# Conditioned two-layer attention: ten second-layer groups send their output by transfers, and GpSimd inverts and divides for them

## The reference

```python
def layer0(x, cond):                      # [4, 512, 256]
    xm = rms(x) * (1 + scale(cond)) + shift(cond)
    q, k, v = split(xm @ w_qkv)           # rope on q and k
    o = softmax(q @ k.T / 4) @ v          # per head
    return o @ w_out + x

def layer1(x, emb, mask):
    xn = layer_norm(x)
    q, k, v = xn @ q_w + q_b, xn @ k_w + k_b, (xn @ v_w + v_b) * mask
    y = softmax(q @ k.T - 1e6 * (1 - mask)) @ v
    h = layer_norm(y) * (1 + scale(emb)) + shift(emb)
    return x + silu(h) @ out_w + out_b
```

## Time and profile before

| | us |
|---|---|
| median of 3 runs (490.25 to 492.41) | 490.78 |
| the profiled execution | 490.88 |
| its span, first to last instruction | 488.7 |
| PE busy | 477.4 |
| DVE busy | 385.4 |
| ACT busy | 342.1 |
| POOL busy | 313.7 |

### The profile page before, as it was taken

The page is one execution under the profiler, slowest core; times in us unless marked ns, Lnnn a source line. Parts: engine busy times, 40 slices in busy tenths (PEclk is TensorE's granted clock), DMA queues, the critical chain, the costliest instruction groups (busy, mean ns, idle before and its releaser), DMA issues.

```text
span 488.7 us, 9702 instructions
## 1 busy us (share of the span) xinstructions
PE 477.4 (98%) x3197; PEld 179.5 (37%) x3197; DVE 385.4 (79%) x989; ACT 342.1 (70%) x677; POOL 313.7 (64%) x445
## 2 busy tenths in 40 slices
PE   7999899999999999999999999999999999999996
PEld 3553322322443325332443335334333323333234
DVE  3767896999886796958886698866899999999124
ACT  2662467898667785968667785876787788777853
POOL 5569976899885996789755791859990055005501
PEclk9999999999999999999999999999999999999999
DMA  7775157454522465216502361113311121111011
GB/s 251 201 202 192 45 152 250 112 150 128 150 61 65 129 178 151 62 33 181 154 19 69 113 179 45 46 45 113 106 46 44 45 89 45 44 46 45 1 44 44
DMA packets 41577, 49.79 MB, mean 102 GB/s; under 512 B 12388, under 2 KB 34036, under 8 KB 41272
## 3 DMA queue, kind: packets, MB, share of 16 engines
q1 hardware_dynamic: 33336, 31.84, 21.8%
q0 software_dynamic: 7904, 16.03, 11.3%
q10 hardware_dynamic: 288, 1.31, 0.8%
HBM read 27.62 MB, written 19.01 MB: 95 GB/s over the span
## 4 chain that ended last, share of the span: by engine, by line
PE 79%; DVE 12%; POOL 3%; issue 2%; ACT 1%; DVEq 0%; POOLq 0%; ACTq 0%
PE bank L596 20%; PE bank L642 12%; PE bank L570 12%; PE bank L579 11%; PE bank L558 9%; DVE masked L955 7%; PE bank L653 6%; PE bank L670 5%; DVE row_max L958 2%; PE bank L627 2%; POOL XN L930 1%; PE bank L611 1%; PE bank L604 1%; ACT probs L780 1%; PE bank L727 1%
## 5 line engine op out<-in xcount | busy, mean ns | idle before, releaser
L780 ACT ACTIVATE probs<-bank 128x512 f32<-128x512 f32 x512 | 269.2, 601 | 71.1 <-PE bank L570 70.3
L958 DVE TENSOR_REDUCE row_max<-bank 128x1 f32<-128x512 f32 x256 | 159.4, 681 | 34.0 <-PE bank L579 33.7
L579 PE MATMUL bank<-k_s,q_s 64*128 64x512 f16 x512 | 178.3, 382 | 2.0 <-DVE row_max L958 1.2
L955 DVE CUSTOM_DVE_ANT_0 masked<-bank,mask_bias 128x512 bf16<-128x512 f32 x256 | 161.8, 687 | 19.3 <-PE bank L579 18.7
L558 PE MATMUL bank<-q_s,k_s 64*128 64x512 f16 x512 | 151.5, 380 | 0.3
L570 PE MATMUL bank<-shift,kx 64*128 64x512 f16 x512 | 148.8, 376 | 0.0
L596 PE MATMUL bank<-probs,v_aug 128*17 128x512 f32 x1024 | 135.4, 598 | 0.7 <-ACT probs L780 0.7
L579 PEld LDWEIGHTS bank<-k_s,q_s 64*128 64x128 f16 x512 | 46.2, 93 | 156.1 <-DVE row_max L958 70.2
L642 PE MATMUL bank<-xT,wqkv 128*128 128x512 f32 x128 | 59.6, 605 | 1.1 <-DVE xT L1096 0.6
L1236 POOL TENSOR_SCALAR scaled<-row_max 128x16 f32<-128x16 f32 x30 | 7.7, 256 | 81.4 <-DVE row_max L955 45.1
L570 PEld LDWEIGHTS bank<-shift,kx 64*128 64x128 f16 x512 | 46.8, 95 | 33.6 <-DMA shift<-shift_rows 0.4
(11 more groups left out here) (123 smaller groups left out, 478.7 us busy)
## 6 DMA issues: line engine op xcount, KB each, us to landing
q_s<-q_parts SPq DMA_DIRECT2D x32, 256.0 KB, 3.0
k_s<-k_parts SPq DMA_DIRECT2D x32, 256.0 KB, 3.7
k_parts<-parts POOLq DMA_DIRECT2D x62, 128.0 KB, 3.0
q_parts<-parts POOLq DMA_DIRECT2D x60, 128.0 KB, 3.1
X<-in_x SPq DMA_DIRECT2D x4, 512.0 KB, 7.2
O<-oT SPq DMA_DIRECT2D x64, 32.0 KB, 2.2
roped<-inverses SPq DMA_DIRECT2D x16, 128.0 KB
y<-X SPq DMA_DIRECT2D x7, 256.0 KB, 2.2
```

Source lines behind the costliest of these rows:

```text
L579: nc.tensor.matmul(bank, m.q_s[slot][rows, i, queries], m.k_s[slot][rows, i, :], start=True, stop=True).then_inc(q.d_made, 1)
L780: act.activation(m.probs[k][:, h, :], bank, ACT.Exp, scale=1.0 if s >= B * NG else float(DH) ** -0.5)\
L955: dve.tensor_tensor_reduce(m.masked[D["max", n, k, h] % ND][:, :], bank, m.mask_bias[:, b, :], 1.0, LOWEST, ALU.add, ALU.max, to)\
L958: dve.tensor_reduce(to, bank, AX.X, ALU.max).then_inc(q.d_done, 1)
```

## The change

The last six groups (26 to 31) stay as they are. Groups 16 to 25 (up to the new `SENT` = 26) go the way of layer 0: sums, raw output and inverses by SP's transfers.

- **Pool** inverts, with a power of -1 over 128x16 (`invert`), in place of DVE's reciprocal, and divides each chunk of two groups in place in `raw`. Its list from shift 19 on is written out anew: ten inverts and five divisions among the shifts, splits, bias additions and normalisations; silu and the bias additions are cut into halves in some places.
- **PE** turns a divided chunk back with four transposes (`turn_back`, pieces `back`, in ring A), so five times four in place of ten times four. **ACT** copies the result to `tokens`, which lies in the memory of the conditioning weights. **DVE** no longer inverts and multiplies for these groups; its statistics wait for the copy of the last turn back.
- **SP** issues per group seven transfers more (one of sums, four of raw output, one each of inverses out and in), and waits in `inverses_out` for Pool's invert, and in `inverses_in` for the write to have landed.
- **Pieces** move: back turns stand at steps 20 (tile 1), 21 (tile 3, ahead of the value products of the last sequence, which were in step 20), 23 (tile 3), 25 (tile 2) and 28 (tile 2). The two w_out halves of sequences 0 and 1 are paired, in step 25 and 28, tile 3; the turns of normalised tokens are a step later (23 and 27), as are two of the statistics (21 and 25). QKV chunks 2 and 3 of the last sequence in layer 0 are paired in step 1, tile 2.

```diff
+SENT = LAYER + NG * (B - 2) + NG // 2
...
-    1: (qk(0, 3, 2), (), qk(0, 3, 3), ()),
+    1: ((), (), qk(0, 3, 2, 3), ()),
...
-PIECES[20] = ((), qk(1, LAST, 2, 3), (), v(1, LAST))
-PIECES[22] = (*one(turn("f1", 0)), (), ())
-PIECES[23] = ((), (), y(1, 0)[:1], ())
-PIECES[24] = ((), (), (), y(1, 0)[1:])
-PIECES[26] = (*one(turn("f1", 1)), (), ())
-PIECES[27] = ((), (), y(1, 1)[:1], ())
-PIECES[28] = ((), (), (), y(1, 1)[1:])
...
+PIECES[20] = ((), qk(1, LAST, 2, 3) + (("back", 0, 0),), (), ())
+PIECES[21] = ((), (), (), (("back", 0, 1),) + v(1, LAST))
+PIECES[23] = (*one(turn("f1", 0)), (), (("back", 1, 0),))
+PIECES[25] = ((), (), (("back", 1, 1),), y(1, 0))
+PIECES[27] = (*one(turn("f1", 1)), (), ())
+PIECES[28] = ((), (), (("back", 2, 0),), y(1, 1))
...
-for _b in range(B - 1):
-    STATISTICS[20 + NG * _b, 3] = ("f1", _b)
+for _b, _s in enumerate((21, 25, 28)):
+    STATISTICS[_s, 3] = ("f1", _b)
...
-OUT_AT = {25: 0, 29: 1, 32: 2}
+OUT_AT = {26: 0, 29: 1, 32: 2}
...
-        if op == "output" and k == 2 and s > LAYER:
+        if op == "output" and k == 2 and s > SENT:
...
-        if op == "output" and k == 3 and 0 < s <= LAYER:
+        if op == "output" and k == 3 and 0 < s <= SENT:
...
+        m.tokens = [m.wc[:, 2 * i:2 * i + 2, :].rearrange("p k n -> p (k n)").rearrange("p (t c) -> p t c", c=C)
+                    for i in range(2)]
...
+    def turn_back(piece):
+        _, b, c = piece
+        bank = a_free(A[piece])
+        pe.wait_ge(q.divided, normalised(B + b, c))
+        for t in range(TPB):
+            last = nc.tensor.transpose(bank[:, t * P:(t + 1) * P], m.raw[b % 2][:, c, t * P:(t + 1) * P], m.ident[:, :])
+        last.then_inc(q.a_made, 1)
...
+    def back(piece):
+        _, b, c = piece
+        bank = made(A[piece])
+        if b >= 2:
+            act.wait_ge(q.xn_made, TPB * NORMAL.index(("f1", b - 2)))
+        act.activation(m.tokens[b % 2][:, :, c * P:(c + 1) * P], bank.rearrange("p (t n) -> p t n", n=P), ACT.Copy)\
+            .then_inc(q.a_done, 1)
...
-        if s == LAYER:
-            dve.wait_ge(q.inv_out, 16 * LAYER)
-        if g == 0 and pu < B + 2:
-            dve.wait_ge(q.divided, normalised(pu - 2, CT - 1))
-        if g == 0 and pu >= B + 2:
+        if s == SENT:
+            dve.wait_ge(q.inv_out, 16 * SENT)
+        if s == SENT or g == 0:
...
-        if s > LAYER:
+        if s > SENT:
...
-        dve.tensor_tensor(m.O[pu % 2][:, :, g * G * DH:(g + 1) * G * DH].rearrange("p t (h d) -> p t h d", d=DH),
+        dve.tensor_tensor(m.tokens[pu % 2][:, :, g * G * DH:(g + 1) * G * DH].rearrange("p t (h d) -> p t h d", d=DH),
...
-            dve.wait_ge(q.d_done, D["output", NG * (B + b) + NG - 1] + 1)
-            statistics(kind, b, lambda t: m.O[b % 2][:, t, :])
+            dve.wait_ge(q.a_done, max(A[piece] for piece in A if piece[:2] == ("back", b)) + 1)
+            if NG * (B + b) + NG > SENT:
+                dve.wait_ge(q.d_done, D["output", NG * (B + b) + NG - 1] + 1)
+            statistics(kind, b, lambda t: m.tokens[b % 2][:, t, :])
...
-    def add_bias(b, j):
+    def add_bias(b, j, tiles=range(2)):
...
-        for t in (2 * j, 2 * j + 1):
+        for i in tiles:
+            t = 2 * j + i
...
-    def divide(b, c):
...
-        use = USES.index(("f0", b))
-        pool.wait_ge(q.output_out, group_out(NG * b + 2 * c + 1))
-        pool.wait_ge(q.inv_in[c], 32 * (b + 1))
-        await_read(pool, q, use - 2)
-        pool.tensor_tensor(m.xT[use % 2][:, c, :], m.raw[b % 2][:, c, :], m.inverse[c][:, :], ALU.mult)\
-            .then_inc(q.divided, 1)
+    def divide(pu, c):
...
+        layer, b = divmod(pu, B)
+        pool.wait_ge(q.output_out, group_out(NG * pu + 2 * c + 1))
+        pool.wait_ge(q.inv_in[c], 32 * (pu + 1))
+        to = raw = m.raw[b % 2][:, c, :]
+        if layer == 0:
+            use = USES.index(("f0", b))
+            await_read(pool, q, use - 2)
+            to = m.xT[use % 2][:, c, :]
+        pool.tensor_tensor(to, raw, m.inverse[c][:, :], ALU.mult).then_inc(q.divided, 1)
...
+    def invert(s):
...
+        pool.wait_ge(q.sums_in, 16 * (s + 1))
+        pool.wait_ge(q.inv_out, 16 * s)
+        pool.tensor_tensor(m.inv_sum[:, :, :, :].rearrange("p t h w -> p (t h w)"), m.sums[s % 2][:, :], m.minus_one[:, :],
+                           ALU.pow).then_inc(q.inv_made, 1)
...
-    normalise(LAST)
-    add_output_bias(LAST)
-    add_bias(LAST - 1, 0)
-    add_bias(LAST - 1, 1)
-    negate(NG * LAST + 9)
-    for i in range(4):
-        split(B + LAST, i)
...
-    for b in range(LAST):
-        negate(NG * (B + b) + 6)
-        rstd("f1", b)
-        normal("f1", b)
-        if b == 0:
-            add_bias(LAST, 0)
-        negate(NG * (B + b) + 7)
-        if b == 0:
-            add_bias(LAST, 1)
-        for h in range(CT):
+    def silu(b, halves=range(CT)):
+        for h in halves:
...
-        for n in (NG * (B + b) + 8, NG * (B + b) + 9):
-            if n in POOL_SHIFTS:
-                negate(n)
...
+    pool.wait_ge(q.one_made, 1)
+    invert(16)
+    invert(17)
+    normalise(LAST)
+    divide(B, 0)
+    add_output_bias(LAST)
+    add_bias(LAST - 1, 0)
+    invert(18)
+    add_bias(LAST - 1, 1)
+    negate(21)
+    split(B + LAST, 0)
+    invert(19)
+    split(B + LAST, 1)
+    negate(22)
+    divide(B, 1)
+    invert(20)
+    split(B + LAST, 2)
+    split(B + LAST, 3)
+    negate(23)
+    rstd("f1", 0)
+    normal("f1", 0)
+    invert(21)
+    negate(24)
+    invert(22)
+    divide(B + 1, 0)
+    silu(0, (0,))
+    negate(25)
+    silu(0, (1,))
+    invert(23)
+    add_bias(LAST, 0, (0,))
+    negate(26)
+    divide(B + 1, 1)
+    add_bias(LAST, 0, (1,))
+    invert(24)
+    add_bias(LAST, 1)
+    negate(27)
+    rstd("f1", 1)
+    normal("f1", 1)
+    invert(25)
+    negate(28)
+    divide(B + 2, 0)
+    silu(1)
+    negate(29)
+    negate(GROUPS - 2)
+    rstd("f1", 2)
+    normal("f1", 2)
+    negate(GROUPS - 1)
+    silu(2)
...
-        if b >= 2:
+        if b >= B + 2:
+            sp.wait_ge(q.a_made, A["back", b - 2 - B, g // 2] + 1)
+        elif b >= 2:
...
-        if 0 < s <= LAYER:
+        if 0 < s <= SENT:
...
-        if 0 < s <= LAYER:
+        if 0 < s <= SENT:
...
-        if 0 < s <= LAYER:
+        if 0 < s <= SENT:
...
+        if LAYER < s <= SENT:
+            inverses_in(s - 1)
```

More of the change, by code:

```diff
@@ L278, in chunk_rows, with normalised @@
     return slice(G * DH * (g % 2), G * DH * (g % 2 + 1))
-def normalised(b, c):
-    return CT * b + c + 1
+def normalised(pu, c):
+    return CT * pu + c + 1
 def await_shift(engine, q, n):
@@ L384, in build @@
         m.minus_half = sb("minus_half", [P, NT])
+        m.minus_one = sb("minus_one", [P, KT * G])
         m.stats = sb("stats", [P, NT, 6])
@@ L408, in build @@
         m.k_dram = nc.dram_tensor("k_parts", [LAYERS * B, H, 2, 2, DH, S], F16, kind="Internal").ap()
-        m.inv_dram = nc.dram_tensor("inverses", [B * NG, G, S], F32, kind="Internal").ap()
+        m.inv_dram = nc.dram_tensor("inverses", [SENT, G, S], F32, kind="Internal").ap()
         def sem(name):
@@ L430, in build @@
         q.inv_made = sem("inv_made")
+        q.one_made = sem("one_made")
         q.xn_made = sem("xn_made")
@@ L752, in tensor @@
                 turn_tokens(piece)
+            if piece[0] == "back":
+                turn_back(piece)
             if piece[0] == "qk":
@@ L909, in scalar @@
                 tokens(piece)
+            if piece[0] == "back":
+                back(piece)
             if piece[0] == "qk":
@@ L1113, in last_batch @@
     def last_batch():
-        O = m.O[LAST % 2]
+        O = m.tokens[LAST % 2]
         steps = [TPB]
@@ L1173, in vector @@
                 negate(n)
-        if op == "sums":
+        if op == "sums" and at[0] < LAYER:
             invert(*at)
@@ L1180, in vector @@
                 for t in range(TPB):
-                    dve.bn_stats(m.last_stats[:, t, 0, :], m.O[LAST % 2][:, t, 0:EARLY]).then_inc(q.last_step, 1)
+                    dve.bn_stats(m.last_stats[:, t, 0, :], m.tokens[LAST % 2][:, t, 0:EARLY]).then_inc(q.last_step, 1)
         if op == "statistics":
@@ L1211, in normal @@
             await_turned(pool, q, NORMAL[n - 2])
-        src = m.O[b % 2] if kind == "f1" else m.X[:, TPB * b:TPB * b + TPB, :]
+        src = m.tokens[b % 2] if kind == "f1" else m.X[:, TPB * b:TPB * b + TPB, :]
         for t in range(TPB):
@@ L1327, in gpsimd @@
     pool.memset(m.minus_half[:, :], -0.5).then_inc(q.ident_made, 1)
+    pool.memset(m.minus_one[:, :], -1.0).then_inc(q.one_made, 1)
     pool.memset(m.ident[:, :], 0.0).then_inc(q.ident_made, 1)
```

## The result

The changed kernel takes 497.64 us (median of six runs, 496.11 to 499.34), the kernel before 490.83 beside it: a ratio of 1.013, 95% interval 1.0097 to 1.0163. It is 6.8 us slower where 2.8 us of gain were forecast, and it lies outside the range. The profiled execution took 496.11 with a span of 494.3, so it is 5.2 us above the profiled execution of before.

The account below looks back on a forecast made before the run. The prediction took PE's summed work to set each step, with DVE close behind. From 490.88 us it took 4.4 for the sum without waits and added 1.6 for new waits: 488.0 us, range 485.8 to 490.8.

Parts of the forecast that it names:

- The sum without waits: Whole kernel: transposes out -6.3, turns back +3.15, pairs -0.63, DVE -0.64, together -4.4 us.
- The pairs and DVE's 0.32: Two pieces paired save 0.21, three times; DVE's 0.32 excess is given back in two steps with statistics and a residual.
- The prediction's bound of 0.6: ACT's copies of turned-back chunks cost 0, unless one delays a score bank: then at most 0.6 us each.
- The power: Pool's power over 128x16 takes 3.0 us, extrapolated from 0.71 for two columns and 1.04 for four.
- land about 1.9 after issue: SP's transfers of sums, which Pool's powers wait for, land about 1.9 us after issue.
- PE turns it 1.36 after the mark: PE turns every shift 1.36 us after ACT's step-end mark, so shifts must start by 0.5 after it.
- just in time: Pool's splits end 14.1 us after mark 20 and step 21 takes 14.2, so shift 23 meets its slot.
- power 22 covers it: The read back of inverses lands later than other transfers, but Pool's power 22 runs meanwhile, hiding that.
- The wait for chunk (1, 0): Step 23, tile 3: PE wants the chunk at t + 16.9, Pool divides it by t + 18.4; wait some 1.5 us.
- Slower: Rival, chance 0.07: powers of 4.2 us make shifts and chunks late, 7.5 us in waits, 494 us; decides from about 3.9.
- A longer wait: Rival, chance 0.18: each 0.3 us more in a power or landing costs about 0.9; 489.7 to 490.7 us.
- No wait: Rival, chance 0.25: powers of 2.5 us or less, so PE finds chunk (1, 0) divided; 486.4 us.

Follow-up runs that it names:

- e1: The changed kernel with the ten inverts given back from Pool to DVE as reciprocals: 487.4 us, ratio 0.9931 to the kernel before.
- e8: e1's kernel, line for line, measured once more for a narrower interval: 487.74 us, ratio 0.995 to the kernel before.
- e2: The changed kernel with Pool's power of 128x16 replaced by a copy of 128x16, all waits kept: 488.23 us, ratio 0.9946 to the kernel before.
- e7: The kernel before with only the pairing of w_out halves and of QKV chunks 2 and 3, no transfers: 489.83 us, ratio 0.9983.
- e5: e3's kernel with group 16's read back issued behind group 17's sums and chunk (1, 0)'s turn a step later: 488.89 us, ratio 0.9949 to the kernel before.
- e3: The changed kernel with step 20's QKV pair and back turn moved from tile 1 to tile 2: 492.94 us, ratio 1.0039 to the kernel before.
- e6: The kernel before with two unused powers of 128x16 ahead of shift 23 on Pool: 495.51 us, ratio 1.0088.

## Why the prediction was wrong, point by point

**The sum without waits: mechanism right, up to 1 us too large.** -4.4 was forecast; e1 and e8, in which only small waits are left, give -3.4 and -3.1 by the medians. Between the marks of 16 and 28 e1 saves 3.16 and e2, which leaves the ten reciprocals off DVE as the change does, 3.53, where the terms for that stretch, all but the first pair, made 4.2. Three terms were mis-sized. A group's transposes beside other pieces don't cost 0.63: in e1 step 18 went from 17.72 to 17.30 and step 19 from 15.07 to 14.64, so 0.42 and 0.43, 0.4 less together. The pairs and DVE's 0.32 were booked as 0.42 + 0.64 for the steps 23, 24, 27 and 28; e7, which has both in it, saves 0.35 + 0.34, so 0.37 less. And the turns back had no price for their bank: in step 25 of e1 the turn stood 0.44 us for a bank of ring A that ACT's exponentials still held. (The prediction's bound of 0.6 was for the other way round, a copy that delays a score bank.) PE's timeline in e1:

```profile
391.14 0.63 PE L643 MATMUL bank<-ident,O 128*128 128x128 f32 x4 [0.44 <-ACT probs L798]
```

Together 0.4 + 0.37 + 0.44 = 1.2, more than the 0.7 to 1.0 that is missing; what came out better than booked is not followed here.

**The power: right.** 3.0 forecast, 2.93 measured. The Trainium skill ("GPSIMD Engine Reference", 3.1 Elementwise) gives about 2.6 cycles per element for two-input arithmetic, an estimated 42 cycles for 16 columns; the prediction made 0.2 to 0.3 us of it. The row above of 2931 ns is about ten times that and does not agree with it. The page's advice to leave elementwise work to DVE held: the reciprocal took 245 ns there in e1.

**Sums that "land about 1.9 after issue": the first step that failed.** The row is one whose read back had gone 6.0 us ahead on the queue (266.82 and 272.83). In the kernel before no engine waited for sums, so no row shows how they land close behind a read back; the change has Pool wait for them there. The same issue took 4.3 us at 302.01, 0.73 us behind a read back; e5 turned the order and it took 1.97. So shift 20 was 1.2 us late. The plan gave "about a microsecond left" in these slots, so a landing 2.4 longer had to show.

**"PE turns it 1.36 after the mark": the second, and the dearest.** That row is from step 23, right behind the mark of step 22, where tile 1 has no pieces. In step 20 tile 1 has a QKV pair and a turn back ahead of the shift's turn, which came 5.4 after the mark. The trace of before had it: with the QKV pair alone the turn of that step stood 5.0 behind the mark at 329.25. PE's timeline there:

```profile
334.25 0.23 PE L604 MATMUL bank<-ident,neg_max 128*32 128x128 f16 x1
```

The prediction listed SP's order, but applied it to power 21 alone: SP's shift, raw output and inverses of step 20 all stand behind that turn. From there "just in time" for shift 23 became 2.40 us of idle time, and chunk (0, 1), held to be divided 6 us ahead, a wait of 0.64. The write of the inverses was part of it: the prediction took 1.42 us for it, and it landed 4.06 us after its issue. The kernel before had longer ones too, as its next write shows, 2.77 on SP's timeline:

```profile
282.73 0.58 SPq L1567 DMA_DIRECT2D inverses<-inv_sum  x1
...
285.50 0.62 SPq L1576 DMA_DIRECT2D roped<-inverses  x1
```

e3 undoes this step alone and gets 4.7 us back.

**"power 22 covers it", the longer landing of the read back: wrong for chunk (0, 1).** In Pool's list that division stands ahead of power 20, with nothing to do but wait, and Pool stood 5.47 us.

**The wait for chunk (1, 0): right in place and chain, too small by the first step again.** It was 2.00 against 1.5, and 3.04 in e3, where the clock and shift 23 no longer delay PE. In e3, counted from the mark of step 21 at 358.80, power 21 ends at 10.0 (forecast 10.1) and the sums leave at 12.2 (12.2), but they land in 3.80 us and not 1.9, 0.71 behind a read back. SP's and Pool's timeline in e3:

```profile
370.25 0.62 SPq L1649 DMA_DIRECT2D roped<-inverses  x1
370.96 0.61 SPq L1623 DMA_DIRECT2D sums<-oT  x1
374.76 2.93 POOL L1357 TENSOR_TENSOR inv_sum<-sums,minus_one 128x16 f32<-128x16 f32 x1 [5.02 <-DMA sums<-oT]
```

Chunk (1, 1), held to be 0.5 to 2.5 us ahead, was waited for too, 0.56.

**The clock: not in the sum at all.** Of the profiled execution's excess 1.7 us are this. The runs' mean clocks were 0.990 to 0.997; a stretch like the one shown takes 3.4 / 2 / 494 = 0.0034 off the mean, so most runs, at 0.993, would have had two of them. Where the second one lay was not seen, since only the run at 0.997 has a trace; e8 has one behind a wait in step 13, so it can lie there too. At 1.7 each, it is about as much as the profiled execution, 496.11, lies below the median of 497.64.

**The rivals.** "Slower" was given for powers of 4.2, and decided from 3.9. It came out slower with powers of 2.93: the mechanism, Pool late and PE waiting at shifts and turns, is the rival's, but the power was no longer than forecast: what it could not carry was the landings and SP's queue. "A longer wait" had the landings in it ("from a stretch with other traffic") but priced them at 0.9 per 0.3 us up to 490.7 only. "No wait" is e1's and e2's case, 487.4 and 488.2 and not 486.4.

**What stays open.** Why the inverses' write took 4.06 us at 340.58 and 1.61 at 338.96 in e3: in the slow case four transfers of Pool's were issued beside it (339.87 to 342.3). The ten traces point at these. Where the read back waits for nothing but the write (the first sequence and every second group), all 31 writes that SP issued while Pool was issuing four transfers took 2.44 to 4.06 us to the read back, and of the other 104 writes 92 took less than 1.9. But no run took these transfers away. And the wait in step 13 for the landing of a shift: 1.03 us in the changed kernel, 1.9 in e8, none in e1, though e1 and e8 are the same kernel. It is not the change's, as e6, the kernel before with a late shift in step 22, has 1.60 of it.

## What to carry to other kernels

A landing time belongs to a place in a queue: take it from a row that has the same transfer as close ahead of it and the same traffic beside it, and where there is none, bound it by the longest row. Where an order is serial, walk each queue item by item through the step that has most pieces, not through a bare one; a slack of a microsecond is none. On a kernel that keeps PE busy, price an idle gap above its own length, since the clock can fall after it.

## What the runs showed of the hardware

**A small transfer behind a large one.** The sums (8 KB) took 4.3 us from issue to Pool's start with a read back (128 KB) issued 0.73 ahead, 3.80 with one 0.71 ahead (e3) and 1.97 with it behind (e5). One more place in the changed kernel, SP's and Pool's timeline:

```profile
373.25 0.62 SPq L1649 DMA_DIRECT2D roped<-inverses  x1
374.75 0.61 SPq L1623 DMA_DIRECT2D sums<-oT  x1
377.70 2.93 POOL L1357 TENSOR_TENSOR inv_sum<-sums,minus_one 128x16 f32<-128x16 f32 x1 [5.21 <-DMA sums<-oT]
```

Issued 1.50 us behind a read back the sums took 2.95, and 4.35 behind (383.19 and 387.54, power at 389.53) 1.99. In each case they were there 4.4 to 5.0 us after the read back's issue or 2.0 after their own, whichever was later. The Trainium skill ("DMA: Bandwidth & Descriptors", Queues, rings and completion order) has a transfer's signal land only after every earlier write of that DMA engine; these rows agree with it.

**A power costs by the column on Pool,** 0.71, 1.04 and 2.93 us for 2, 4 and 16 columns, where a copy of 16 takes 0.198 and a subtraction 0.22.

**The clock falls after short gaps, and not always.** It stood at 0.50 or 0.51 after idle times of 2.40 (changed kernel), 2.81 (e6) and 1.90 (e8), in a PE that was busy before; in e3's profiled execution, after 3.04, it did not fall, nor after 2.00 in the changed kernel, nor after the 1.60 of step 13 in e6. What decides between them no run here shows.
